# One projection issued ahead of the scores in a windowed-attention loop

## The chip, the cores and the metric

The kernel runs on one core of a Trainium2 chip. The core has five engines that run side by side and meet at semaphores: TensorE for matrix products (its weight loads are listed apart), VectorE, ScalarE, GpSimd, and SyncE, which only issues transfers. The metric is device time in microseconds (us) of one execution, as the median of several.

## The reference

The reference is a decoder of four blocks, each made of a self-attention, a cross-attention and a feed-forward layer, on x of shape 8 x 128 x 128. The change lies in one layer alone, `l1_ffn`, which is itself a small transformer of depth 2 with local attention. Cut to what matters here, each depth computes:

```
h = shift_token(x)                      # second half of the features comes from the token before
q, k, v = split(h @ wqkv)               # 8 heads of 64
q, k = l2norm(q) * qs, l2norm(k) * ksc  # per head
q, k = rotary_xpos(q, k)
o = local_attention(q, k, v)            # windows of 64, each sees itself and the one before
x = x + o @ wo
x = x + gated_ffn(shift_token(x))       # layernorm, w1 (2 x 341), gelu gate, w2
```

The norm of q and k stands ahead of the rotation, and the scores q @ k stand behind it, so each group of tokens goes through a long chain of small operations: projection, squares, their sum, the inverse root, the product with it, rotation, transposition, scores, softmax, values, output projection.

## The kernel before

All twelve layers run one after the other. In `layer_l1_ffn` (line 2888 on) the tokens are cut into 8 blocks of 128 for each of the 2 depths. A loop over steps s = 0 to 7 treats block s, and at the same time prepares the blocks behind it. There is no scheduler: on each engine the instructions run in the order in which the code issues them, and an instruction whose semaphore has not come up holds all that is behind it on that engine. What one step does, by engine:

- TensorE: `turn_qk` (transposes of the rotated q and k, line 3044), `score` (two products that lay the band mask into the banks, line 3056, then the score products, line 3062), `project` twice (q and k of block s + 2, line 3028), `turn_out` (3070), `turn_shifted` (3078), `project_values` (3035), `project_out` (3087), `hand` (3098, 3101), `value` (3112).
- ScalarE: the copy of the turned q and k to memory (3269), for which the score products wait; the squares of the q and k of block s + 2 (`square`, 3208); the copy of the turned output (3216); the exponentials (3281); copies of values and handed rows.
- VectorE: `unite` (3315), which multiplies q and k of block s + 1 with their inverse norms and by that empties the two projection banks; `divide` (3323, 3327) and `add` (3335) of earlier blocks; the row maxima of the scores (3410) and the subtraction of them (3414); `sum_squares` of block s + 2 (3340, 3345); the sum of the rotated halves (3350); `measure` (3356 to 3364).
- GpSimd: the rotation of block s + 1 (2965, 2967) behind `unite`; then the inverse root of the sums of squares of block s + 2 (2998), for which the next step's `unite` waits.

`project(d, b, n)` writes q (n = 0) or k (n = 1) of a block into one bank each, `QK_BANKS[n]`. There is one such bank for q and one for k. So the product for block s + 2 may not start before `unite` has read the one of block s + 1 out of it: that is the wait in lines 3026 and 3027, and `unite` of block s + 1 stands first in VectorE's step s.

At depth 1, step 0 differs: seven dummy products (`keep_clock_bf`, line 134) stand between `turn_qk` and `score`, and a `turn_x` behind the two projections.

Of the kernel before, what the change touches and what calls it, by code (L numbers as in the profile page):

```python
# [26 lines left out]
B = 8  # L27
# [139 lines left out]
def for_heads(bias, n=4):  # L167

    return bias.unsqueeze(1).broadcast_to([bias.shape[0], n, bias.shape[1]])
# [312 lines left out]
class SmallHeads:  # L482
# [44 lines left out]
    def by_head(self, ap):  # L527
        return ap.rearrange("p (h k) -> p h k", h=4)
# [2359 lines left out]
def layer_l1_ffn(core, tag, w):  # L2888
# [54 lines left out]
    with nc.Block(tag, no_gpsimd_drain=True) as block:  # L2943
# [63 lines left out]
        def _(pe):  # L3007

            def turn_x(d, h):
                bank = X_BANK[d][h]  # L3010
                if d == 0:
                    norm.pe(pe, h, bank)
                    pe.wait_ge(norm.turned.sem, norm.half(norm.turned, h))
                else:
                    pe.wait_ge(joined.sem, joined.at(2 * (d - 1) + h))
                    pe.wait_ge(taken.sem, taken.at(hand_at(d, -1)))
                    for b in range(B // 2 * h, B // 2 * (h + 1)):
                        t = nc.tensor.transpose(ps[bank][:, b % 4 * P:(b % 4 + 1) * P], res[:, b, :], core.ident[:, :])
                    t.then_inc(x_turned.sem, x_turned.up())

            def project(d, b, n):
                g = 8 * d + b
                if b % 4 == 0:
                    pe.wait_ge(x_low.sem, x_low.at(2 * d + b // 4))
                    pe.wait_ge(x_high.sem, x_high.at(2 * d + b // 4))
                if g > 0:
                    pe.wait_ge(united.sem, united.at(2 * (g - 1) + n))
                nc.tensor.matmul(ps[QK_BANKS[n]][:, :], core.xnT[:, b * P:(b + 1) * P], wqkv[d][:, n * BANK:(n + 1) * BANK],  # L3028
                                 start=True, stop=True).then_inc(qk_made.sem, qk_made.up())

            def project_values(d, b):
                g = 8 * d + b
                if b == 1:
                    pe.wait_ge(values_out.sem, values_out.at(g - 1))
                nc.tensor.matmul(ps[A_BANKS[0]][:, :], core.xnT[:, b * P:(b + 1) * P], wqkv[d][:, 2 * BANK:3 * BANK],
                                 start=True, stop=True).then_inc(values_made.sem, values_made.up())

            def turn_qk(g):
                for n in range(2):
                    pe.wait_ge(added_half.sem, added_half.at(2 * g + n))  # L3040
                    if g > 0:
                        pe.wait_ge(exped.sem, exped.at(2 * (g - 1) + n))
                    for i in range(4):
                        t = nc.tensor.transpose(ps[T_BANKS[n]][:, i * P:(i + 1) * P], rotated[:, n, i * P:(i + 1) * P],
                                                core.ident[:, :])
                    t.then_inc(qk_turned.sem, qk_turned.up())

            def score(d, b):
                g = 8 * d + b
                pe.wait_ge(values_out.sem, values_out.at(min(g + 1, 8 * d + 7)))  # L3050
                if b >= 3:
                    pe.wait_ge(taken.sem, taken.at(hand_at(d, b - 3)))
                if d > 0 and b == 0:
                    pe.wait_ge(joined.sem, joined.at(2 * d - 1))
                for n in range(2):
                    nc.tensor.matmul(by_head(ps[A_BANKS[n]][:, :]), core.ident_bf[:, :], for_heads(core.band_bf[:, :]),
                                     start=True, stop=False)
                pe.wait_ge(qk_out.sem, qk_out.at(2 * g + 1))
                for i in range(4):
                    for n in range(2):  # L3060
                        rows = slice(K * n, K * n + K)
                        m = nc.tensor.matmul(ps[A_BANKS[n]][:, i * P:(i + 1) * P], qkT[rows, 0, i, :], qkT[rows, 1, i, :],
                                             start=False, stop=(i == 3))
                        if i == 3:
                            m.then_inc(scores.sem, scores.up())

            def turn_out(g):
                pe.wait_ge(normed.sem, normed.at(2 * g + 1))
                for i in range(4):
                    t = nc.tensor.transpose(ps[O_BANKS[0]][:, i * P:(i + 1) * P],  # L3070
                                            o.rearrange("p h k -> p (h k)")[:, i * P:(i + 1) * P], core.ident[:, :])
                t.then_inc(turned_out.sem, turned_out.up())
# [43 lines left out]
            def up(d, h, i):  # L3116
                n, m = chunk_at(d, h, i), WIDTHS[i]
                if n >= 2:
                    pe.wait_ge(gated.sem, gated.at(n - 2))
                pe.wait_ge(taken.sem, taken.at(hand_at(d, (5, 8)[h])))  # L3120
                for part in range(2):
                    mm = nc.tensor.matmul(ps[GATED_BANKS[h][i][part]][0:m, :],
                                          w1[d][:, part * HID + i * P:part * HID + i * P + m], xn2T[:, half(h)],
                                          start=True, stop=True)
                mm.then_inc(up_made.sem, up_made.up())

            def down(d, h):
                pe.wait_ge(gated.sem, gated.at(chunk_at(d, h, CHUNKS - 1)))
                for t in range(4):
                    for i, m in enumerate(WIDTHS):  # L3130
                        mm = nc.tensor.matmul(ps[DOWN_BANK[h]][:, t * P:(t + 1) * P], hT[h][0:m, i, t * P:(t + 1) * P],
                                              w2[d][0:m, i, :], start=(i == 0), stop=(i == CHUNKS - 1))
                mm.then_inc(down_made.sem, down_made.up())
# [5 lines left out]
            for d in range(DEPTH):  # L3139
                if d == 0:  # L3140
                    for b in range(2):
                        for n in range(2):
                            project(d, b, n)
                        project_values(d, b)
                else:
                    turn_x(d, 0)
                    up(d - 1, 1, 0)
                    project(d, 0, 0)
                    project(d, 0, 1)
                    up(d - 1, 1, 1)  # L3150
                    project_values(d, 0)
                    up(d - 1, 1, 2)
                    down(d - 1, 1)
                    project(d, 1, 0)
                    project(d, 1, 1)
                    project_values(d, 1)
                for s in range(B):
                    g = 8 * d + s
                    turn_qk(g)
                    if s == 0 and d > 0:  # L3160
                        core.keep_clock_bf(O_BANKS[1], 7)
                    score(d, s)
                    if s + 2 < B:
                        project(d, s + 2, 0)
                        project(d, s + 2, 1)
                    if s == 0 and d > 0:
                        turn_x(d, 1)
                    if s >= 1:
                        turn_out(g - 1)
                    turn_shifted(g)  # L3170
                    if s + 2 < B:
                        project_values(d, s + 2)
                    if s >= 1:
                        project_out(d, g - 1)
                    if s >= 2:
                        hand(d, s - 2, NEXT_BANK)
                    value(g)
                last = 8 * d + 7
                up(d, 0, 0)
                turn_out(last)  # L3180
                hand(d, 6, LAST_BANK)
                up(d, 0, 1)
                project_out(d, last)
                up(d, 0, 2)
                hand(d, 7, LAST_BANK)
                core.keep_clock_bf(O_BANKS[0], 6)
                down(d, 0)
                hand(d, 8, LAST_BANK)
# [1138 lines left out]
```

## Time and profile before

| | |
|---|---|
| time, median of 3 runs | 1264.51 us (1263.1 to 1265.53) |
| the profiled execution's own time | 1265.53 us |
| its span | 1263.6 us |
| busy over the span: TensorE products | 1132.3 us (90%) |
| TensorE weight loads | 788.6 us (62%) |
| VectorE | 687.9 us (54%) |
| ScalarE | 533.4 us (42%) |
| GpSimd | 472.0 us (37%) |
| mean granted TensorE clock | 0.954 of full |

The span is from the first to the last instruction of the profiled execution; its own time has some 2 us around that. The busy shares are means over twelve layers with different limits, so they say little about one loop. The loop that is changed runs from 519 us (depth 0) and from 627 us (depth 1) after the start of the span. Transfers are few there: the layer's weights were loaded before.

### The profile page before, as it was taken

Reading aid. Unit: us, or ns where it says so; the run is one execution under the profiler, and the core shown is the slowest. Engines: PE = TensorE matmul, PEld = TensorE weight load, DVE = VectorE, ACT = ScalarE, POOL = GpSimd, SP = SyncE. Lnnn points to the kernel's source line nnn. Section 1 sums busy time; section 2 is a strip of 40 time slices with the busy share of each in tenths; the row PEclk is TensorE's granted clock in tenths of the full one; section 3 lists DMA queues with packets and bytes.
Section 4 is the critical chain, followed back from the end, with each engine's and each line's share of the span. In section 5 each row is a group of like instructions: output and inputs, shape, how many; then the busy total and the mean of one; then the engine's idle time right before and its main releaser. Section 6 shows DMA issues by size and latency. Waiting matters only on the chain. (4 is left out here: it accounts for less than half of the span.)

```text
span 1263.6 us, 22906 instructions
## 1 busy us (share of the span) xinstructions
PE 1132.3 (90%) x8793; PEld 788.6 (62%) x8793; DVE 687.9 (54%) x2110; ACT 533.4 (42%) x1374; POOL 472.0 (37%) x547
## 2 busy tenths in 40 slices
PE   5999989999867886798899899989999999988987
PEld 5877867577642254477467666745567775556765
DVE  5555552354449945586478467638722146846402
ACT  5434332366546642355445453304443323443332
POOL 7959730122345622785478250012000012031404
PEclk9999999899996788899999999999999998999989
DMA  5000050532029001000000000000011100010312
GB/s 178 1 5 2 1 217 1 167 85 68 2 104 267 20 2 43 1 1 1 1 1 1 1 10 2 2 11 25 22 55 34 50 16 1 2 38 21 113 37 56
DMA packets 51628, 52.54 MB, mean 42 GB/s; under 512 B 19552, under 2 KB 42336, under 8 KB 50496
## 3 DMA queue, kind: packets, MB, share of 16 engines
q1 hardware_dynamic: 50496, 48.97, 12.4%
q0 software_dynamic: 1024, 2.10, 0.8%
q8 instruction: 71, 1.16, 0.4%
q14 instruction: 37, 0.30, 0.1%
HBM read 43.85 MB, written 7.21 MB: 40 GB/s over the span
## 5 line engine op out<-in xcount | busy, mean ns | idle before, releaser
L471 POOL TENSOR_TENSOR ln_rstd<-ln_ve,ln_half 128x4 f32<-128x4 f32 x28 | 28.5, 1019 | 286.6 <-DVE ln_ve L446 286.4
L664 ACT ACTIVATE scratch<-bank 128x512 f32<-128x512 f32 x96 | 52.3, 595 | 77.1 <-PE bank L555 77.1
L619 DVE TENSOR_REDUCE scratch<-bank 128x4 f32<-128x512 f32 x96 | 61.5, 682 | 16.6 <-PE bank L539 8.8
L1252 ACT ACTIVATE scratch<-bank 128x512 f32<-128x512 f32 x64 | 38.2, 596 | 66.5 <-PE bank L1208 66.4
L2065 POOL TENSOR_TENSOR scratch<-scratch 128x512 f32<-128x512 f32 x32 | 33.2, 1039 | 86.4 <-DVE scratch L2247 86.4
L1218 PEld LDWEIGHTS bank<-weights,scratch 128*128 128x128 f32 x512 | 59.5, 192 | 7.2 <-issue 7.2
L2998 POOL TENSOR_TENSOR scratch<-scratch 128x16 f32<-128x16 f32 x16 | 51.7, 3231 | 32.0 <-DVE scratch L3345 31.9
L1271 DVE SCALAR_TENSOR_TENSOR x_res<-bank,scratch,x_res 128x128 f32<-128x128 f32 x64 | 18.0, 344 | 82.3 <-PE bank L1218 82.3
L625 DVE TENSOR_TENSOR scratch<-bank,scratch 128x512 f32<-128x512 f32 x96 | 61.3, 679 | 0.0
L1208 PE MATMUL bank<-xnT,weights 128*128 128x512 f32 x128 | 59.5, 608 | 0.7 <-ACT xnT L1241 0.7
L1218 PE MATMUL bank<-weights,scratch 128*128 128x128 f32 x512 | 59.6, 275 | 0.0
L539 PE MATMUL bank<-scratch 32*128 32x512 f32 x192 | 52.3, 632 | 1.5 <-DVE scratch L625 1.4
L555 PEld LDWEIGHTS bank<-ident,scratch 128*128 128x128 f32 x384 | 42.0, 141 | 17.6 <-DVE scratch L625 10.6
L555 PE MATMUL bank<-ident,scratch 128*128 128x128 f32 x384 | 51.8, 278 | 0.6 <-DVE scratch L625 0.6
L2200 ACT ACTIVATE scratch<-bank,scratch 128x128 f32<-128x128 f32 x128 | 45.0, 387 | 3.4 <-DVE scratch L2271 3.4
L3551 POOL TENSOR_TENSOR scratch<-scratch 128x1024 f32<-128x1024 f32 (+5 forms) x48 | 42.9, 894 | 3.8
L3546 POOL TENSOR_TENSOR scratch<-scratch 128x2048 f32<-128x2048 f32 x8 | 36.2, 4523 | 16.6 <-DVE weights L1759 16.1
L1505 ACT ACTIVATE scratch<-bank 128x512 f32<-128x512 f32 (+1 forms) x48 | 25.7, 543 | 38.6 <-PE bank L1425 37.5
L1208 PEld LDWEIGHTS bank<-xnT,weights 128*128 128x128 f32 x128 | 23.7, 195 | 25.0 <-issue 23.6
L2271 DVE TENSOR_REDUCE scratch<-bank 128x4 f32<-128x512 f32 x32 | 20.6, 686 | 34.2 <-PE bank L2144 34.2
L3208 ACT ACTIVATE scratch<-bank 128x512 f32<-128x512 f32 x32 | 19.1, 598 | 46.5 <-PE bank L3028 46.5
L3028 PE MATMUL bank<-weights,xnT 128*128 128x512 f32 x64 | 33.4, 646 | 5.8 <-DVE scratch L3315 5.7
(591 smaller groups left out, 2942.1 us busy)
## 6 DMA issues: line engine op xcount, KB each, us to landing
scratch<-conv_kernels SPq DMA_DIRECT2D x8, 1024.0 KB, 11.0
weights<-e_l_ffn_w SPq DMA_DIRECT2D x20, 256.0 KB, 3.0
scratch<-e_l_ffn_w SPq DMA_DIRECT2D x4, 1024.0 KB, 15.3
values<-scratch SPq DMA_DIRECT2D x8, 512.0 KB, 2.7
scratch<-values SPq DMA_DIRECT2D x8, 512.0 KB, 4.4
weights<-w_l_ffn SPq DMA_DIRECT2D x1, 3698.0 KB, 12.4
scratch<-e_l_ffn_w SPq DMA_DIRECT2D x4, 768.0 KB, 6.9
weights<-w_l_attn SPq DMA_DIRECT2D x1, 2560.5 KB, 9.3
```

Of the source, the lines that this page charges most:

```text
L539: s = self.nc.tensor.matmul(self.by_head(self.core.ps[n % 4][:, :]), self.qT[rows, b * P:(b + 1) * P], self.km[rows, :, b * P:(b + 1) * P] ...
L555: t = self.nc.tensor.transpose(self.core.ps[4 + n % 2][:, i * P:(i + 1) * P], self.shift[:, n % 4, i * P:(i + 1) * P], self.core.ident[:, :])
L619: self.nc.vector.tensor_reduce(self.top[:, n % 4, :], self.by_head(self.core.ps[n % 4][:, :]), AX_X, ALU.max, negate=True).then_inc(self.t ...
L625: self.nc.vector.tensor_tensor(self.by_head(self.shift[:, n % 4, :]), self.by_head(self.core.ps[n % 4][:, :]), self.top[:, n % 4, :].unsqu ...
L664: self.nc.scalar.activation(self.prob_of(n), self.by_head(self.core.ps[4 + n % 2][:, :]), ACT.Exp, scale=scale) \
L1208: nc.tensor.matmul(ps[UP_BANKS[i]][:, :], wa[e % 2][:, i * P:(i + 1) * P], core.xnT[:, half(h)], start=True, stop=True).then_inc(up_made.s ...
L1218: mm = nc.tensor.matmul(ps[Y_BANKS[u % 3]][:, t * P:(t + 1) * P], hT[h][:, i, t * P:(t + 1) * P], wb[e % 2][:, i, :], start=(i == 0), stop ...
L1252: nc.scalar.activation(hT[u % 2][:, i, :], ps[UP_BANKS[i]][:, :], act_func) \
L2200: a = nc.scalar.activation(prob[:, r, 4 * i + j, :], ps[S_BANKS[i]][:, j * P:(j + 1) * P], ACT.Exp, bias=top[:, i, j:j + 1], accum_out=tot ...
L2998: nc.gpsimd.tensor_tensor(rn, ss, power, ALU.pow).then_inc(rooted.sem, rooted.up())
L3546: link(tt(prod, z, wa[:, a].unsqueeze(1).broadcast_to([P, R, 2 * N]), ALU.mult))
L3551: link(tt(out, prod[:, :, 0:h], prod[:, :, h:2 * h], ALU.add))
```

## The change

One of the two projections of block s + 2, that of q, is issued ahead of `score` instead of behind it. The one of k stays where it was. Nothing is added or taken away; in step 6 and 7 there is no projection and nothing changes. It holds for steps 0 to 5 of both depths, 12 places.

```diff
                     turn_qk(g)
                     if s == 0 and d > 0:
                         core.keep_clock_bf(O_BANKS[1], 7)
+                    if s + 2 < B:
+                        project(d, s + 2, 0)
                     score(d, s)
                     if s + 2 < B:
-                        project(d, s + 2, 0)
                         project(d, s + 2, 1)
                     if s == 0 and d > 0:
                         turn_x(d, 1)
```

TensorE's order at depth 0, step 0, before. `bank` is a PSUM bank, `scratch` the layer's working memory, `xnT` the turned tokens, `weights` the layer's weights; one row of a projection or a 128x128 product is one call of the code.

```order
L3044 MATMUL bank<-ident,scratch 128x128 x8
L3056 MATMUL bank<-band_bf,ident_bf 128x512 x2
L3062 MATMUL bank<-scratch 128x128 x8
L3028 MATMUL bank<-weights,xnT 128x512 x2
L3078 MATMUL bank<-ident,scratch 128x128 x8
L3035 MATMUL bank<-weights,xnT 128x512
L3112 MATMUL bank<-scratch 128x65 x8
```

And now, the same engine and step:

```order
L3044 MATMUL bank<-ident,scratch 128x128 x8
L3028 MATMUL bank<-weights,xnT 128x512
L3056 MATMUL bank<-band_bf,ident_bf 128x512 x2
L3062 MATMUL bank<-scratch 128x128 x8
L3028 MATMUL bank<-weights,xnT 128x512
L3078 MATMUL bank<-ident,scratch 128x128 x8
L3035 MATMUL bank<-weights,xnT 128x512
L3112 MATMUL bank<-scratch 128x65 x8
```

The product of line 3028 for q went ahead of the mask products and the scores; the one for k is behind them. Steps 1 to 5 of depth 0 and of depth 1 move in the same way.

TensorE's order at depth 1, step 0, where the dummy products of line 134 stand, before:

```order
L3044 MATMUL bank<-ident,scratch 128x128 x8
L134 MATMUL bank<-key_bias,ident_bf 128x512 x7
L3056 MATMUL bank<-band_bf,ident_bf 128x512 x2
L3062 MATMUL bank<-scratch 128x128 x8
L3028 MATMUL bank<-weights,xnT 128x512 x2
L3018 MATMUL bank<-ident,scratch 128x128 x4
```

And now:

```order
L3044 MATMUL bank<-ident,scratch 128x128 x8
L134 MATMUL bank<-key_bias,ident_bf 128x512 x7
L3028 MATMUL bank<-weights,xnT 128x512
L3056 MATMUL bank<-band_bf,ident_bf 128x512 x2
L3062 MATMUL bank<-scratch 128x128 x8
L3028 MATMUL bank<-weights,xnT 128x512
L3018 MATMUL bank<-ident,scratch 128x128 x4
```

The projection for q went behind the dummies and ahead of the mask products and scores. On the other engines no instruction moved.

## Rows read from the trace of the kernel before

**Rows 1.** Busy time by engine, us and (instructions): depth 0, steps 0 to 7.
```profile
core 0: us, PE busy (x) PEld busy (x) DVE busy (x) ACT busy (x) POOL busy (x), PEclk, DMA share, GB/s
519.00:595.00 76.00, 69.07 (x524) 53.07 (x524) 57.98 (x134) 37.40 (x78) 56.21 (x45) 1.00 0.00 1
```

**Rows 2.** Timeline (start, us busy, engine, line, tiles), depth 0, step 5: VectorE, GpSimd.
```profile
569.33 1.29 DVE L3315 TENSOR_TENSOR scratch<-bank,scratch 128x512 f32<-128x512 f32 x2 [0.51 <-POOL scratch L2998]
...
571.42 0.28 DVE L3335 TENSOR_TENSOR scratch<-scratch,bank 128x128 f32<-128x128 f32 x1
...
571.77 1.29 DVE L3410 TENSOR_REDUCE scratch<-bank 128x4 f32<-128x512 f32 x2
...
574.33 1.22 DVE L3340 TENSOR_REDUCE scratch<-scratch 128x16 f32<-128x1024 f32 x1
...
575.84 3.28 POOL L2998 TENSOR_TENSOR scratch<-scratch 128x16 f32<-128x16 f32 x1 [1.49 <-DVE scratch L3345]
...
579.15 1.29 DVE L3315 TENSOR_TENSOR scratch<-bank,scratch 128x512 f32<-128x512 f32 x2 [0.68 <-POOL scratch L2998]
```

**Rows 3.** Timeline, depth 0, step 5: TensorE and ScalarE.
```profile
568.80 1.05 PE L3044 MATMUL bank<-ident,scratch 128*128 128x128 f32 x8
...
569.45 1.07 ACT L3269 COPY scratch<-bank 128x512 f32<-128x512 f32 x2 [1.67 <-PE bank L3044]
...
570.58 1.16 PE L3062 MATMUL bank<-scratch 64*128 64x128 f32 x16 [0.29 <-ACT scratch L3269]
...
571.67 1.98 PE L3028 MATMUL bank<-weights,xnT 128*128 128x512 f32 x4
...
573.49 0.60 PE L3070 MATMUL bank<-ident,scratch 128*128 128x128 f32 x4
573.69 0.60 ACT L3208 ACTIVATE scratch<-bank 128x512 f32<-128x512 f32 x1 [0.26 <-PE bank L3028]
...
578.62 1.04 PE L3044 MATMUL bank<-ident,scratch 128*128 128x128 f32 x8
```

**Rows 4.** Timeline, depth 0, step 0 and the start of step 1.
```profile
519.73 1.28 PE L3044 MATMUL bank<-ident,scratch 128*128 128x128 f32 x8 [1.04 <-DVE scratch L3350]
...
522.46 1.29 DVE L3315 TENSOR_TENSOR scratch<-bank,scratch 128x512 f32<-128x512 f32 x2 [2.17 <-POOL scratch L2998]
...
523.21 1.98 PE L3028 MATMUL bank<-weights,xnT 128*128 128x512 f32 x4 [0.36 <-DVE scratch L3315]
...
523.67 1.28 DVE L3410 TENSOR_REDUCE scratch<-bank 128x4 f32<-128x512 f32 x2
...
530.89 1.29 DVE L3315 TENSOR_TENSOR scratch<-bank,scratch 128x512 f32<-128x512 f32 x2 [2.17 <-POOL scratch L2998]
```

**Rows 5.** Timeline, depth 1: step 0, start of step 1, step 5's reduction.
```profile
630.30 1.29 DVE L3315 TENSOR_TENSOR scratch<-bank,scratch 128x512 f32<-128x512 f32 x2 [2.17 <-POOL scratch L2998]
...
631.87 0.59 PE L3056 MATMUL bank<-band_bf,ident_bf 128*128 128x512 bf16 x2
...
632.39 1.16 PE L3062 MATMUL bank<-scratch 64*128 64x128 f32 x16
...
633.58 1.29 DVE L3410 TENSOR_REDUCE scratch<-bank 128x4 f32<-128x512 f32 x2 [1.99 <-PE bank L3062]
...
641.63 1.29 DVE L3315 TENSOR_TENSOR scratch<-bank,scratch 128x512 f32<-128x512 f32 x2 [2.17 <-POOL scratch L2998]
...
682.52 1.29 DVE L3410 TENSOR_REDUCE scratch<-bank 128x4 f32<-128x512 f32 x2
```

**Rows 6.** Busy time by engine in two stretches around a fall of the clock.
```profile
624.90:628.30 3.40, 1.51 (x7) 0.54 (x6) 2.61 (x4) 1.18 (x3) 1.42 (x2) 0.99 0.00 0
628.30:631.70 3.40, 3.40 (x11) 1.69 (x12) 1.29 (x2) 1.13 (x2) 2.60 (x2) 0.51 0.02 5
```
**Rows 7.** Timeline, depth 0 before step 0: a projection at the low clock.
```profile
513.20 3.78 PE L3028 MATMUL bank<-weights,xnT 128*128 128x512 f32 x4 [5.09 <-DVE scratch L3315]
```

**Rows 8.** Line L3062's own view: idle before it by releaser, us and times.
```profile
  ACT scratch L3269: 16.2, 30
```

## The prediction

> **What bounds the loop now.** I read the busy times first, then the timeline of one step, engine by engine, then the two odd steps at the heads of the depths. Through depth 0's steps TensorE is busy for 69.07 of 76 us, or 91%, at a granted clock of 1.00; VectorE has 76%, GpSimd 74%, the weight loads 70% [rows 1]. By the first figure TensorE is the engine to relieve, and the edit would do that: it puts a product where TensorE stands before the scores.
>
> The timeline says otherwise. Call T the start of a step's `unite` (L3315). In depth 0's step 5 T is 569.33, and the next is 579.15. Between them stands one chain: `unite` to 570.62, `divide`, `add` to 571.70, the row maxima from 571.77, the subtraction, the sum of squares at 574.33, then GpSimd's power from 575.84 to 579.12, which is what the next `unite` waited for [rows 2]. The step is 9.82 us long, and VectorE and GpSimd account for all of it by turns. The row maxima start 0.07 after `add` ends and 1.19 after the first score product (570.58) [rows 2, 3]. So in this step scores and `add` come almost together: the scores have no slack towards VectorE. TensorE is nearly a ring of its own: from row maxima to the next transposes (578.62) 6.85 us, from transposes to row maxima 2.97 (568.80 to 571.77) [rows 2, 3]. Both rings need 9.8 us.
>
> **What the projection waits for.** The bank of q is emptied by the first half of `unite`, the first thing of VectorE's step. In step 0 `unite` starts at 522.46 and the waiting product at 523.21: T + 0.75 [rows 4]. The copies of the turned q and k, which the scores wait for now, are ready at 570.52, T + 1.19 (569.45 + 1.07), and the scores start at T + 1.25 [rows 3]. The projection can't run in the hole for nothing: the hole is from about T + 0.8 to T + 1.25, and the product needs more. Two projections and the passage to `turn_out` take 573.49 - 571.67 = 1.82, so one takes 0.91 [rows 3].
>
> **The new step.** TensorE does matmuls in the order of the code, so what is queued behind the waiting projection is the mask pair, the scores, and behind these VectorE's row maxima. From T: 0.75 for the wait, 0.91 for q's projection, 0.43 for the mask pair, 1.19 from the first score product to the row maxima. Sum: row maxima at T + 3.28. The 0.43 is the pair's 0.59 less the tail of the last; the other bound is 0.52, from the start of the pair to the scores [rows 5]. With it the sum is 3.37. A projection may be 0.86, if 0.1 of the 1.82 is the passage from the scores' weights to the first product's, an estimate; then the sum is 3.23. I take 3.28.
>
> From row maxima to the next T: 579.15 - 571.77 = 7.38 in step 5, and 530.89 - 523.67 = 7.22 in step 0 [rows 2, 4]. The difference is that in step 5 the sum of squares waits for ScalarE's second square (573.69 + 0.60 = 574.29, sum at 574.33) [rows 2, 3]. With the row maxima late this wait goes: k's projection is then done before the subtraction. So 7.22 holds, and a full step is 3.28 + 7.22 = 10.50 us instead of 9.82.
>
> Does TensorE permit 10.50? Its own ring would be: row maxima + 6.85 gives the next transposes at T + 10.13, done by 11.17 (1.04), against q's projection at T + 11.25. It comes first by a little. The ring's old hole, where it stood for the copies, is filled, but it isn't the longer ring any more.
>
> Early steps lose more, because there row maxima came soon after T: in step 0 at T + 1.21 (no `divide` or `add` before them) [rows 4].
>
> **The sum, depth 0.** Before, from step 0's T to step 5's row maxima: 571.77 - 522.46 = 49.31. After: 5 x 10.50 + 3.28 = 55.78. Loss 6.47; bounds 6.1 and 7.0 with 3.23 and 3.37. Steps 6 and 7 have no projection, and TensorE leads them: row maxima + 6.85 + 2.97, as before. Nothing is given back there.
>
> **The sum, depth 1.** In step 0 the dummy products hold the mask pair until 631.87, T + 1.57, so the bank has long been free when the projection's turn comes, and the row maxima are late by the projection alone: 633.58 + 0.91 = 634.49. Before, 641.63 - 633.58 = 8.05 followed; that stays, because `turn_x` behind both projections is where it was. The next T is 642.54. Then 4 x 10.50 + 3.28 to step 5's row maxima: 687.82 against 682.52 [rows 5]. Loss 5.30; bounds 5.0 and 5.8.
>
> Together 11.8 us. No transfer is issued by the moved step, and what follows the layer starts when its last product is joined, so it moves along whole.
>
> **The clock.** In depth 0's step 0 TensorE has the transposes from 519.73 to 521.01 and stood until 519.73; now it would stand again from 521.0 to 523.21 [rows 4]. In 624.90 to 628.30 it was busy 1.51 of 3.40 us, and then the granted clock went from 0.99 to 0.51 for the next 3.4 us, its lower level of 1.2 GHz [rows 6]. The new stretch from 519.7 to 523.2 has 1.3 busy in 3.5, less than that, so a fall is likelier than not. At the low clock two projections took 3.78 against 1.98 us [rows 7, 3]: half the speed. If it caught the projection and the mask pair (0.91 + 0.43 at full speed) it would cost 1.3; with the scores' 1.19 too, 2.5; if it doesn't fall, 0. I take 1.3. In the other steps TensorE stands for about 1 us in 10.5, in two pieces, and the clock should stay. The Trainium skill (TensorE: Matmul & The Clock Gate, HAM oscillation) ties the fall to gaps in which TensorE is idle throughout, longer than the one here. By that rule this term is 0 and the sum 11.8. The trace speaks against it: the fall at 628.3 followed a stretch with 1.51 us of work in it.
>
> **Forecast.** 11.8 + 1.3 = 13.1 us. Against the profiled execution's own 1265.53 us (2 us around its span of 1263.6) that is 1278.6; against the median of 1264.51, 1277.6. The execution read was the slowest of three by 1 us, inside the spread.
>
> **Rivals.**
>
> A. As forecast but with no fall of the clock: 1264.5 + 11.8 = 1276.3; with the low bounds (11.1) 1275.6. For it: I have one fall to go by, and where the stretches of idleness fall may differ by execution. 30%, against 48% for the forecast itself.
>
> B. The clock falls in more steps, since TensorE's share drops from 91% to about 85% and its pauses are longer. Each fall costs 1.3 to 2.5; with three more it is about 1283. Against it: depth 0's step 0 of before, with 0.36 us of pause and a longer one behind it, kept 1.00 [rows 1, 4]. 8%.
>
> C. Faster. TensorE is the bound, and its wait before the scores is filled with useful work. That wait is 16.2 us in 30 cases, weight loads and products counted apart [rows 8]; of the product's own hole about 0.44 us can be saved in a step (0.29 at least, by what stood before the scores) [rows 3]. In 12 steps that is 5.3 us at the most: 1259.2. It decides if q's projection has its bank free when the transposes end, that is if `unite` ended its first half before; in step 5 the transposes end at 569.85 and that half at about 570.0, and the ring of VectorE and GpSimd would have to have slack, which rows 2 deny. The Trainium skill (Perfetto Trace Analysis, Identifying the Most-Contended Engine) says to work on the engine with the highest occupancy, but to judge TensorE by its weight loads and not by its products' busy time. By the products' 91% rival C would hold; by the loads' 70%, below VectorE's 76%, it falls, and the trace agrees with the second half of the rule. 5%.
>
> D. No change: the lateness of the scores is absorbed, since the sum of squares, and with it GpSimd's power, could be limited by the squares and not by the row maxima, and q's square comes earlier now. Then 1264.5, within 2.5. Against it: the sum of squares is behind the row maxima in VectorE's order, and the maxima can't precede the scores. 9%.
>
> **The numbers.** Faster by over 0.2% is C: 0.05. Within 0.2%, some 2.5 us, which is about what these runs can tell from no change, is D: 0.09. Slower is the forecast, A and B: 0.86. The range: from below A, with a few steps costing less than 0.68 (TensorE or VectorE making up half of it in six steps, 2 us; with A's low bound that gives 1273.5, and I allow 2 more), to the forecast with the high bounds of 12.8 and 2.5, 1279.8, and one more fall of the clock: 1271.5 to 1282.
>
> **What would show it.** In the changed profile: row maxima (L3410) waiting for the scores (L3062) in all of steps 0 to 5, at T + 3.2 to 3.4; T to T 10.5 us; a product of L3028 waiting for `unite` in 11 steps; no wait of the scores for the copies (L3269) in those steps; the mask pair right behind a projection. Depth 0's stretch from 522.46 to step 5's row maxima should be 55.8 us or some 57, and depth 1's 57.5. The prediction is wrong if T to T stays at 9.8, if the product starts before T + 0.75, or if the lateness of step 5 is gone by step 7.

## The result

| | before | changed |
|---|---|---|
| median | 1263.19 us (1262.57 to 1265.53, 5 runs) | 1275.11 us (1272.66 to 1277.42, 5 runs) |
| profiled execution's own time | 1265.53 us | 1275.4 us |
| its span | 1263.6 us | 1273.6 us |
| mean granted clock | 0.954 | 0.955 |

The changed kernel takes 1.0095 times as long, with an interval of 1.0078 to 1.0112: 11.9 us slower. The forecast was 13.1 us slower and 1277.6 us.

The page's busy times hardly moved. Products, weight loads, VectorE, ScalarE and GpSimd of the changed kernel:

```profile
PE 1133.1 (89%) x8779; PEld 785.4 (62%) x8793; DVE 688.0 (54%) x2110; ACT 534.7 (42%) x1374; POOL 471.8 (37%) x547
```

The time went into standing, so it has to be looked for in a step. In the changed kernel lines behind 3162 have a number one higher: `unite` is 3316, the row maxima are 3411, the copy of the turned q and k is 3270; in the variants further down they move by a few more. This is the timeline of depth 0, step 5 (start, us busy, engine, line, tiles, idle before), the answer to [rows 2, 3], up to the next `unite`:

```profile
577.14 1.04 PE L3044 MATMUL bank<-ident,scratch 128*128 128x128 f32 x8
...
577.50 1.29 DVE L3316 TENSOR_TENSOR scratch<-bank,scratch 128x512 f32<-128x512 f32 x2 [0.34 <-POOL scratch L2998]
...
578.24 0.30 PEld L3028 LDWEIGHTS bank<-weights,xnT 128*128 128x128 f32 x2 [0.29 <-DVE scratch L3316]
578.24 1.12 PE L3028 MATMUL bank<-weights,xnT 128*128 128x512 f32 x2
...
579.20 0.59 PE L3056 MATMUL bank<-band_bf,ident_bf 128*128 128x512 bf16 x2
...
579.73 1.16 PE L3062 MATMUL bank<-scratch 64*128 64x128 f32 x16
...
580.92 1.29 DVE L3411 TENSOR_REDUCE scratch<-bank 128x4 f32<-128x512 f32 x2 [1.06 <-PE bank L3062]
...
582.87 1.25 PE L3078 MATMUL bank<-ident,scratch 128*128 128x128 f32 x8 [0.48 <-DVE scratch L3415]
...
587.77 1.04 PE L3044 MATMUL bank<-ident,scratch 128*128 128x128 f32 x8
...
588.13 1.29 DVE L3316 TENSOR_TENSOR scratch<-bank,scratch 128x512 f32<-128x512 f32 x2 [0.51 <-POOL scratch L2998]
```

A passage, below, is the time from the start of one operation to the start of the next. With T = 577.50: the projection starts at T + 0.74, the mask pair 0.96 later, the scores another 0.53 later, the row maxima 1.19 behind those. They are at T + 3.42 and now stand 1.06 us for the scores. The next T comes 7.21 later. From T to T it is 10.63 us, where it was 9.82.

Step 0 of depth 0 and the start of step 1, the answer to [rows 4]:

```profile
521.97 1.29 DVE L3316 TENSOR_TENSOR scratch<-bank,scratch 128x512 f32<-128x512 f32 x2 [2.17 <-POOL scratch L2998]
522.71 2.08 PE L3028 MATMUL bank<-weights,xnT 128*128 128x512 f32 x2 [2.20 <-DVE scratch L3316]
524.58 1.06 PE L3056 MATMUL bank<-band_bf,ident_bf 128*128 128x512 bf16 x2
525.57 2.08 PE L3062 MATMUL bank<-scratch 64*128 64x128 f32 x16
...
527.68 1.29 DVE L3411 TENSOR_REDUCE scratch<-bank 128x4 f32<-128x512 f32 x2 [4.43 <-PE bank L3062]
...
534.89 1.29 DVE L3316 TENSOR_TENSOR scratch<-bank,scratch 128x512 f32<-128x512 f32 x2 [2.17 <-POOL scratch L2998]
```

TensorE stood 2.20 us and then did projection, mask pair and scores in 1.87 + 0.99 + 2.11 us, where the full step has 0.96 + 0.53 + 1.19: 2.29 us more. The busy times by engine say why; the figure behind POOL's is the granted clock:

```profile
519.00:522.50 3.50, 1.28 (x8) 0.84 (x8) 1.33 (x3) 1.17 (x2) 2.94 (x1) 0.92 0.00 0
522.50:526.00 3.50, 3.29 (x8) 1.23 (x10) 0.76 (x2) 0.60 (x1) 3.26 (x4) 0.50 0.00 0
```

The clock went from 0.92 to 0.50 of full, the level of 1.2 GHz, behind 3.5 us with 1.28 us of products.

Such a stretch is not always followed by a fall. In depth 1's step 1 of the same execution TensorE stood 2.13 us, with 1.48 us of products in 3.5 us, and the granted clock stayed at 1.00:

```profile
652.41 1.13 PE L3028 MATMUL bank<-weights,xnT 128*128 128x512 f32 x2 [2.13 <-DVE scratch L3316]
```

```profile
648.80:652.30 3.50, 1.48 (x14) 1.24 (x13) 1.33 (x4) 1.07 (x2) 2.83 (x1) 1.00 0.00 0
652.30:655.80 3.50, 3.39 (x22) 1.90 (x23) 2.24 (x8) 0.60 (x1) 3.37 (x4) 1.00 0.00 0
```

Depth 1, the answer to [rows 5]: step 0 and the start of step 1.

```profile
639.46 1.29 DVE L3316 TENSOR_TENSOR scratch<-bank,scratch 128x512 f32<-128x512 f32 x2 [2.17 <-POOL scratch L2998]
...
640.65 1.41 PE L3028 MATMUL bank<-weights,xnT 128*128 128x512 f32 x2
...
643.61 1.29 DVE L3411 TENSOR_REDUCE scratch<-bank 128x4 f32<-128x512 f32 x2 [2.86 <-PE bank L3062]
...
651.66 1.29 DVE L3316 TENSOR_TENSOR scratch<-bank,scratch 128x512 f32<-128x512 f32 x2 [2.17 <-POOL scratch L2998]
```

The row maxima are at T + 4.15, where they were at T + 3.28, and the 8.05 us behind them stayed to the hundredth.

| from step 0's T to step 5's row maxima | before | changed | more | forecast |
|---|---|---|---|---|
| depth 0 | 49.31 | 58.95 | 9.64 | 6.47 + 1.3 |
| depth 1 | 52.22 | 58.24 | 6.02 | 5.30 |

The loop lies between two issues of weight transfers on SP. Before and after, that stretch ("the layer" below) reads:

```profile
499.34 0.35 SPq L4210 DMA_DIRECT2D weights<-w_l_attn  x1
732.14 0.34 SPq L4210 DMA_DIRECT2D weights<-w_l_xattn  x1
```

```profile
498.82 0.35 SPq L4211 DMA_DIRECT2D weights<-w_l_attn  x1
...
747.22 0.35 SPq L4211 DMA_DIRECT2D weights<-w_l_xattn  x1
```

232.8 and 248.4 us: 15.6 more, which is the 9.64 + 6.02 of the table. The span grew by 10.0 only. The difference lies in other layers, whose code is the same. The largest piece, between two other issues of weights, before and then changed (busy times by engine, granted clock behind them):

```profile
1033.26:1113.36 80.10, 77.76 (x631) 46.19 (x631) 58.15 (x128) 29.47 (x59) 15.64 (x16) 0.96 0.02 7
```

```profile
1046.68:1123.67 76.99, 74.59 (x630) 44.29 (x631) 58.18 (x128) 29.48 (x59) 15.64 (x16) 1.00 0.02 7
```

The same instructions, 3.1 us shorter, at a granted clock of 1.00 instead of 0.96. Two more layers took 79.3 instead of 80.6 and 118.6 instead of 120.3 us. Over all profiles of this study these three stayed between 77.0 and 80.2, 79.2 and 80.7, 118.6 and 120.3, with and without the change. So the effect is read from the layer, and the ratio stands beside it. What the layer shows is one execution of each kernel; what the timed runs show is 9.9 to 14.2 us, less than the layer's 15.6.

### The profile page after: what moved, and what is told of

Read it like the earlier page. It is cut to its first block and busy times, and to the rows that moved or that the text cites. A ratio compares the mean times of both kernels' runs of the same rounds, so it can differ in the third digit from the quotient of the medians.

```text
span 1273.6 us, 22892 instructions
## 1 busy us (share of the span) xinstructions
PE 1133.1 (89%) x8779; PEld 785.4 (62%) x8793; DVE 688.0 (54%) x2110; ACT 534.7 (42%) x1374; POOL 471.8 (37%) x547
## 3 DMA queue, kind: packets, MB, share of 16 engines
HBM read 43.85 MB, written 7.21 MB: 40 GB/s over the span
## 5 line engine op out<-in xcount | busy, mean ns | idle before, releaser
L1271 DVE SCALAR_TENSOR_TENSOR x_res<-bank,scratch,x_res 128x128 f32<-128x128 f32 x64 | 18.0, 344 | 80.6 <-PE bank L1218 80.6
L3028 PE MATMUL bank<-weights,xnT 128*128 128x512 f32 x64 | 38.4, 695 | 12.3 <-DVE scratch L3316 12.0
```

## The experiments

Each kernel is compared with runs of the kernel before on the same chip; the ratios below are to those. All layers are from one profiled execution of each.

| kernel | layer us | T0 to row maxima 5: depth 0, depth 1 | ratio to before |
|---|---|---|---|
| before | 232.8 | 49.31, 52.22 | |
| changed | 248.4 | 58.95, 58.24 | 1.0095 (1.0078 to 1.0112) |
| e1 depth 0 only | 242.4 | 58.95, 52.24 | 1.0070 (1.0043 to 1.0097) |
| e2 depth 1 only | 238.7 | 49.31, 58.22 | 1.0031 (1.0015 to 1.0048) |
| e3 not in step 0 | 242.7 | 54.45, 57.07 | 1.0062 (1.0032 to 1.0091) |
| e4 dummies in step 0 | 245.2 | 56.67, 57.51 | 1.0103 (1.0031 to 1.0176) |
| e5 mask pair first | 241.2 | 54.26, 55.83 | 1.0054 (1.0037 to 1.0070) |
| e6 both ahead | 260.4 | 64.84, 64.38 | 1.0230 (1.0190 to 1.0270) |
| e9 wait only | 243.6 | 56.12, 56.22 | 1.0078 (1.0044 to 1.0112) |
| e10 changed again | 248.5 | 58.94, 58.22 | 1.0091 (1.0063 to 1.0120) |
| e11 wait and dummies | 236.0 | 51.81, 53.22 | 1.0003 (0.9982 to 1.0023) |
| e12 four dummies | 232.1 | 49.31, 51.58 | 0.9992 (0.9973 to 1.0010) |
| e7 product for power | 226.0 | | 0.9919 (0.9900 to 0.9938) |
| e8 the same, changed | 232.0 | | 0.9971 (0.9945 to 0.9997) |

**e1 and e2: one depth each.** The edit behind `turn_qk`, with `d == 0` in e1 and `d == 1` in e2:

```diff
+                    if s + 2 < B and d == 0:
+                        project(d, s + 2, 0)
                     score(d, s)
-                    if s + 2 < B:
+                    if s + 2 < B and not (d == 0):
                         project(d, s + 2, 0)
+                    if s + 2 < B:
                         project(d, s + 2, 1)
```

Expected of e1: 

> q's projection goes ahead of the scores in depth 0 only. In the two profiles the layer lasted 232.8 us before and 248.4 after; of the 15.6, depth 0 has 9.6 up to step 5's row maxima, 2.4 of it at a fall of the clock in step 0. Theory (the scores are held by the projection's wait and by the product itself, step by step): the layer lasts 242.4, or 240.0 if the clock doesn't fall there, and depth 1 is as before. Rival (something of the layer as a whole, or of other layers, pays): the layer is not between 239.5 and 243.

Expected of e2: 

> q's projection goes ahead in depth 1 only. Theory: the layer lasts 232.8 + 6.0 = 238.8 us, with depth 0 as before, and the two parts add up to the whole 15.6. Rival: the parts don't add up.

Measured: layer + 9.6 and + 5.9, together 15.5, against 15.6 with both. The depth that wasn't changed kept its 52.2 and 49.3. The loss is local and adds up.

**e3: no move in step 0.** As above, with `s > 0` in place of `d == 0`.

Expected: 

> As the changed kernel, but step 0 of both depths is as before. Theory (early steps lose most, since there the row maxima came soon after unite; and the fall of the clock belongs to step 0's long stand): depth 0 loses 5.1 us instead of 9.6, depth 1 5.1 instead of 6.0, the layer lasts 243.0, the clock stays up in depth 0. Rival (each of 12 steps costs the same): 232.8 + 15.6 x 10/12 = 245.8.

Depth 0 lost 5.14 us without a fall of the clock, the five steps' share. Depth 1 lost 4.85 in an unexpected way. In step 0 the clock now stayed up through mask pair and scores, and the row maxima came at T + 1.61 instead of 3.28; in step 1 it fell:

```profile
640.50:644.00 3.50, 2.19 (x20) 1.95 (x19) 1.39 (x3) 1.27 (x3) 3.24 (x1) 1.00 0.00 0
644.00:647.50 3.50, 2.69 (x4) 0.80 (x4) 2.17 (x6) 0.58 (x1) 2.70 (x4) 0.54 0.00 0
```

There T to row maxima was 4.80 us (644.07 to 648.87), 1.38 more than 3.42. With the five steps' share and the 1.67 by which step 0 was shorter (3.28 - 1.61), that is 5.14 - 1.67 + 1.38 = 4.85. So both the pause in step 0 and the first pause of a moved projection are places where the clock may fall. It need not take either: the changed kernel kept 1.00 behind the same pause of 2.13 us in step 1. What decides is not shown.

**e4: the changed kernel with the clock kept up.** Eight dummies between step 0's transposes and the projection:

```diff
+                    if s == 0 and d == 0:
+                        core.keep_clock_bf(O_BANKS[0], 8)
                     if s + 2 < B:
                         project(d, s + 2, 0)
```

Expected: 

> The changed kernel with eight dummy products of 0.21 us into a free bank in depth 0, step 0, between the transposes and the waiting projection. Theory (TensorE's stand of 2.2 us there lets the granted clock fall, which costs 2.4 us): the clock stays at 1.00, step 0's row maxima come at T + 3.4 instead of T + 5.7, the layer lasts 246.1. Rival (the lateness of step 0 is the order alone): 248.4 stays, or more by the dummies.

Busy times around step 0, and its row maxima:

```profile
517.90:521.40 3.50, 2.63 (x15) 1.59 (x16) 1.39 (x3) 1.44 (x3) 3.25 (x1) 1.00 0.00 0
521.40:524.90 3.50, 3.02 (x23) 1.59 (x22) 1.31 (x3) 0.60 (x1) 2.70 (x4) 1.00 0.00 0
```

```profile
521.45 1.29 DVE L3318 TENSOR_TENSOR scratch<-bank,scratch 128x512 f32<-128x512 f32 x2 [2.17 <-POOL scratch L2998]
...
524.88 1.29 DVE L3413 TENSOR_REDUCE scratch<-bank 128x4 f32<-128x512 f32 x2 [2.14 <-PE bank L3062]
```

The granted clock is 1.00 in both, and the row maxima come at T + 3.43, as in a full step, instead of T + 5.71: the fall had cost 2.28. Depth 1, where nothing was edited, had T + 3.43 too instead of 4.15 (its clock stayed up this time), so the layer is 3.2 shorter and not 2.3. The ratio's interval is too wide to show the gain.

**e5: the mask pair ahead of the projection.** `score` is cut in two; `mask` is its waits for the banks and the mask pair:

```diff
                     turn_qk(g)
+                    mask(d, s)
                     if s + 2 < B:
                         project(d, s + 2, 0)
                     score(d, s)
```

Expected: 

> The changed kernel with the mask pair ahead of q's projection, so that it runs while the projection waits. Theory: T to row maxima falls by 0.5 us, but TensorE's own ring (row maxima + 6.85 to the next transposes, then 0.9 + 0.53 + 0.96 + 1.19 to row maxima) is 10.43 us, so a full step goes from 10.63 to 10.43 only and early steps gain 0.5: the layer lasts 245 us. Rival (only the ring of VectorE and GpSimd binds): 11 x 0.5 less, 242.9.

Shorter than theory and rival had it. Depth 0, step 4 and the start of step 5:

```profile
560.61 1.04 PE L3044 MATMUL bank<-ident,scratch 128*128 128x128 f32 x8
560.98 1.29 DVE L3320 TENSOR_TENSOR scratch<-bank,scratch 128x512 f32<-128x512 f32 x2 [0.51 <-POOL scratch L2998]
561.49 0.59 PE L3056 MATMUL bank<-band_bf,ident_bf 128*128 128x512 bf16 x2
561.92 1.02 PE L3028 MATMUL bank<-weights,xnT 128*128 128x512 f32 x2
562.87 1.16 PE L3065 MATMUL bank<-scratch 64*128 64x128 f32 x16
...
564.06 1.29 DVE L3415 TENSOR_REDUCE scratch<-bank 128x4 f32<-128x512 f32 x2 [0.73 <-PE bank L3065]
...
570.91 1.04 PE L3044 MATMUL bank<-ident,scratch 128*128 128x128 f32 x8
```

The mask pair fills the time until `unite` has freed the bank, and the projection starts at T + 0.94 without a wait. Row maxima at T + 3.08; the step is 10.3 us. Here it is TensorE's own ring that sets it: 3.45 from transposes to row maxima and 6.85 back to the transposes. The pause ahead of step 0's projection was shorter by the mask pair (1.77 us), and the clock didn't fall there. In depth 1's step 1 it did, behind a pause of 1.70 us: to 0.83 and then 0.68 in the next two stretches of 3.5 us, and the step took 10.91 where depth 0's took 10.19. The layer is 7.2 us shorter than the changed kernel's. Some 4.8 of it is the order of the work, 0.3 to 0.4 in each of the 12 steps (T to T 10.20 in depth 0's step 0 and 10.29 in its step 4, against 10.64 in both steps of e4); the rest, some 2.4, is clock: 2.3 and 0.7 that the changed kernel lost in the two steps 0, less the 0.7 lost here.

**e6: both projections ahead of `score`.**

```diff
                     if s + 2 < B:
                         project(d, s + 2, 0)
-                    score(d, s)
-                    if s + 2 < B:
                         project(d, s + 2, 1)
+                    score(d, s)
```

Expected: 

> Both projections go ahead of the scores. Theory (the product's own time is paid once more): T to row maxima 4.4 us, a full step 11.6 instead of 10.63, the layer lasts about 259 us. Rival (the wait for unite is what costs, and it is waited for once only; the squares come earlier): 250 or less.

Depth 0, `unite` of one step, its row maxima, and the next `unite`:

```profile
570.91 1.29 DVE L3315 TENSOR_TENSOR scratch<-bank,scratch 128x512 f32<-128x512 f32 x2 [0.51 <-POOL scratch L2998]
...
575.19 1.29 DVE L3410 TENSOR_REDUCE scratch<-bank 128x4 f32<-128x512 f32 x2 [1.92 <-PE bank L3062]
...
582.40 1.29 DVE L3315 TENSOR_TENSOR scratch<-bank,scratch 128x512 f32<-128x512 f32 x2 [0.34 <-POOL scratch L2998]
```

Row maxima at T + 4.28, next T 7.21 later: 11.49. The second product added its passage of 0.86 to every step and took nothing off elsewhere. The dose doubled and the loss went from 15.6 to 27.6. Falls of the clock are in both. Here the row maxima came at T + 7.21 in depth 0's step 0 and T + 5.97 in depth 1's step 1, 2.9 and 1.7 more than 4.28; in the changed kernel 2.3 and 0.7 (T + 4.15 in depth 1's step 0 against 3.43 in e4) are falls. Without them it is 12.6 and 23.0, and the difference is twelve times 0.87. That confirms the term "one projection, once a step, on the chain".

**e7 and e8: GpSimd's power made short.** In line 2998 `pow` becomes `mult` in the kernel before (e7) and in the changed one (e8), so q and k of both are not normed.

```diff
-                        nc.gpsimd.tensor_tensor(rn, ss, power, ALU.pow).then_inc(rooted.sem, rooted.up())
+                        nc.gpsimd.tensor_tensor(rn, ss, power, ALU.mult).then_inc(rooted.sem, rooted.up())
```

Expected of e7: 

> The kernel before with GpSimd's power (3.27 us for 128 x 16) replaced by a product of the same operands in line 2998, so that q and k are not normed. The bank of q is then free long before TensorE's transposes end. Theory: TensorE's ring of 9.82 us stays the step from step 1 on, and only the heads of the depths get shorter, by two powers in depth 0 and one in depth 1 and some 0.7: the layer lasts about 223 us. Rival (the power is on the only binding ring): a step falls to about 8.7 and the layer to 210.

Expected of e8: 

> The changed kernel with the same replacement of the power, against the kernel before with it. The moved projection has its bank free when the transposes end, which is the condition under which my rival C promised a gain. Theory (the product's time is paid ahead of the scores whatever it waits for, and the hole only moves behind them, where TensorE stands for VectorE's subtraction): TensorE's ring is 10.43 us a step against 9.82, and the layer is about 7 us longer than the one of the kernel before with the product. Rival C: the hole before the scores is filled, 0.3 to 0.44 less a step, the layer 4 to 5 us shorter than it.

The operation took 0.59 us instead of 3.27. The full step of e7 stayed at 9.82 us, as the theory has it and the rival (8.7) has not; its layer took 226.0, 3 us more than expected, and these 3 us were not traced. In the later steps `unite` was no longer late: the bank of q is free when the transposes end. Depth 0 of e8, from step 5's transposes to step 6's:

```profile
565.75 1.04 PE L3044 MATMUL bank<-ident,scratch 128*128 128x128 f32 x8
566.63 1.02 PE L3028 MATMUL bank<-weights,xnT 128*128 128x512 f32 x2
567.49 0.59 PE L3056 MATMUL bank<-band_bf,ident_bf 128*128 128x512 bf16 x2
568.02 1.16 PE L3062 MATMUL bank<-scratch 64*128 64x128 f32 x16
...
569.21 1.29 DVE L3411 TENSOR_REDUCE scratch<-bank 128x4 f32<-128x512 f32 x2 [1.17 <-PE bank L3062]
...
571.15 1.25 PE L3078 MATMUL bank<-ident,scratch 128*128 128x128 f32 x8 [0.48 <-DVE scratch L3415]
...
576.06 1.04 PE L3044 MATMUL bank<-ident,scratch 128*128 128x128 f32 x8
```

The condition of rival C is met: the product stands right behind the transposes, the hole before the scores is gone. Yet the step is 10.31 us, against 9.82 in e7, and e8's layer is 6.0 us longer. The reason is in two differences. From transposes to row maxima it is 3.46 us (2.97 before [rows 2, 3]): the product's 0.86 less 0.36 by which the scores had waited for the copies (0.89 from mask pair to scores in e7, 0.53 in e8). And behind the scores one product less brings nothing, since `turn_shifted` (3078) now stands 0.48 us for the subtraction. In the kernel before it had come last behind two projections without a wait, in step 5 with row maxima at 571.77:

```profile
573.93 1.04 PE L3078 MATMUL bank<-ident,scratch 128*128 128x128 f32 x8
574.80 1.02 PE L3035 MATMUL bank<-weights,xnT 128*128 128x512 f32 x2
```

`project_values` (3035) starts 3.03 us behind the row maxima there, and 3.03 in e8. The hole had been moved from ahead of the scores to behind them.

**e9: the wait without the product.** The kernel before, with TensorE waiting for `unite` ahead of `score`, and both projections behind it:

```diff
+                    if s + 2 < B:
+                        pe.wait_ge(united.sem, united.at(2 * (g + 1)))
                     score(d, s)
```

Expected: 

> The kernel before, but TensorE waits ahead of the scores for the first half of unite, as the moved projection does, while the projection itself stays behind the scores. Theory (of a full step's loss nearly all is the product's time, since the wait ends 0.75 us after T and the scores could start at T + 1.25 anyway): row maxima at T + 2.5, a loss of 1.8 in depth 0 and 0.7 in depth 1, the layer lasts 235.3 us, or 237.6 if the clock falls in depth 0's step 0. Rival (it is the wait that costs): 245 or more.

This expectation failed: the layer took 243.6, and that would have spoken for the rival. The stretches say something else. In steps without a fall the row maxima come at T + 2.48 and the step takes 9.85 us, 0.03 more than before. But steps 0 and 1 of depth 0 and step 1 of depth 1 took 12.7, 11.4 and 12.8. Around depth 0's step 1:

```profile
532.50:536.00 3.50, 1.61 (x13) 1.09 (x12) 1.33 (x3) 1.07 (x2) 2.69 (x2) 0.97 0.02 5
536.00:539.50 3.50, 3.50 (x20) 2.46 (x19) 1.97 (x7) 0.00 (x0) 3.50 (x4) 0.55 0.00 0
```

A wait of 1.9 to 2.2 us of TensorE, and the clock at half behind it. Whether that is all of it was asked of e11.

**e11: e9 with the clock kept up.**

```diff
+                    if s == 0 and d == 0:
+                        core.keep_clock_bf(O_BANKS[0], 8)
+                    if s == 1:
+                        core.keep_clock_bf(A_BANKS[1], 8)
                     if s + 2 < B:
                         pe.wait_ge(united.sem, united.at(2 * (g + 1)))
```

Expected: 

> The wait alone ahead of the scores made the layer 243.6 us long, not the 235.3 that I expected. Its trace shows the clock at its lower level in step 0 of depth 0 and in step 1 of both depths, after stands of 2 us. Here eight dummy products into a free bank stand behind the transposes in depth 0's step 0 and in step 1 of both depths, with the same wait. Theory (the wait costs 2.5 us in itself and the rest of its 10.8 is the clock): T to row maxima 2.5 us in these steps, the layer lasts 235.5. Rival (the wait itself costs that much): 242 or more.

In depth 0 the row maxima come at T + 2.48 in step 0 too (524.65 to 527.13) and at T + 2.59 in step 1, and the layer is 236.0. So the wait alone is worth 3.2 us in the layer; the other 7.6 of e9 were the clock. In the changed kernel with the clock kept up (e4) the same layer is 245.2: the product ahead of the scores is worth 9.2. That is rather too little, since e11 has the low clock of the kernel before in depth 1's step 0 (T + 3.29) and e4 has not.

**e10: the changed kernel once more.**

Expected: 

> The changed kernel once more. In the two profiles the layer cost 15.6 us more but the whole span 10.0, since other layers were shorter (the first by 1.3, l3_attn by 1.7, l3_xattn by 3.1, each with a higher granted clock). Theory (these are falls of the clock that come or stay away from one execution to the next): the layer lasts 248.4 again, within 1, while the others vary. Rival (the change shifts them for good): the same layers are shorter again by the same amounts.

Layer 248.5, and the fall in the same place with the same 2.3 us (row maxima at T + 5.71): the loop's numbers repeat on another chip to 0.1 us. Of the three other layers, two did not repeat: they took 80.6 and 78.7 us, where the changed kernel's first profile had 79.3 and 77.0 and the kernel before 80.6 and 80.1. The third took 118.6 again. So the rival, that the change makes the same layers shorter by the same amounts, does not hold as it stands. The timed loss was again smaller than the layer's, 11.6 us against 15.7.

**e12: a smaller fall in the kernel before.** Four dummies instead of seven in depth 1's step 0:

```diff
-                        core.keep_clock_bf(O_BANKS[1], 7)
+                        core.keep_clock_bf(O_BANKS[1], 4)
```

Expected: 

> The kernel before with four dummy products instead of seven at depth 1, step 0, where the row maxima wait 2 us for the scores held up by the dummies. If the clock behaves as before (low for them, back at the first scores), the row maxima come 1.3 us earlier and the layer lasts 231.5. If the dummies are what brings the clock back, the scores run at the lower level and the layer lasts 232.8 or more. Either way the whole moves by less than 0.2%.

The row maxima came at T + 2.64 (3.28 before), the layer took 232.1 (232.8). That lies between the two values of the expectation and settles neither. The ratio's interval holds 1. No version of this study is measurably faster than the kernel before with the same computation.

## Why the prediction was right, and where its sizes were off

**The bound.** Shown. The step is the ring `unite`, row maxima, power, next `unite`, and with the scores late it lengthens by what they are late: T to row maxima 3.42 and 7.21 behind it, where 3.28 and 7.22 were foretold.

**The wait.** T + 0.75 was right: 0.74 in both steps shown. In step 5 no idle time is recorded ahead of the product, since the end of the transposes, 578.18, is only 0.06 before its start; but its weight load stood 0.29 us for `unite`. From transposes to product it is 1.10 us (577.14 to 578.24), and 0.88 in e8, where the bank is free. So `unite` holds the product by some 0.2 us, and TensorE's ring does come "first by a little".

**The passage.** Mis-sized. One projection took 0.96 to the mask pair instead of 0.91, and the pair 0.53 to the scores instead of 0.43. I had 0.52 as the other bound [rows 5] and took the lower one, an overlap for which there was no row with the scores behind the pair. 0.14 a step in eleven steps (all but depth 1's step 0) is 1.5 us. With it both depths lie above the bounds given for them: 9.64 less the clock's 2.29 is 7.35 against 7.0, and 6.02 against 5.8.

**The clock.** The fall came where it was foretold, and behind less work than [rows 6] shows. The size was 2.29 instead of 1.3: it held through the scores. That is near the upper bound of 2.5. The argument was weaker than it looked, though: depth 1's step 1 also had less work (1.48 of 3.5 us) and kept 1.00. And I had written that in the other steps TensorE stands for about 1 us, where it stood 1.28 us in depth 0's step 1 and 2.13 in depth 1's. Neither was followed by a fall in this execution, for no reason that I had given; e3 shows the price, 1.38. The Trainium skill (TensorE: Matmul & The Clock Gate, HAM oscillation) ties the fall to gaps in which TensorE is idle throughout, longer than the one here. In this trace the gap was 2.20 us, in e9 1.89 to 2.20, and the clock fell. By its rule the layer would have been 2.3 us shorter, as e4's step 0 is. The trace doesn't agree.

**Depth 1.** The 0.91 foretold for step 0 was 0.87, and the 8.05 behind it stayed. But the 0.87 is two errors that cancel, and luck. The projection took 1.24 us to the mask pair (640.65 to 641.89), at a clock still partly low, and it started at T + 1.19, where the pair had started at T + 1.57: the fall came later than in the kernel before, so that the transposes ahead of it took 1.28 us instead of 1.72. The rest, 6.02 - 0.87 = 5.15 against 4.39 foretold, is five times the passage's 0.14.

**The sum.** 9.64 + 6.02 = 15.7 in the loop, 13.1 foretold: some 1.6 of the difference for the passages, 1.0 for the clock. The measured 11.9 came nearer to 13.1 than the loop's 15.7 would have, because the rest of the kernel was shorter by 5.6 us in the execution profiled. That closeness is luck, since nothing of it was foretold. In most experiments, too, the timed effect is smaller than the layer's: 11.6 against 15.7 (e10), 8.9 against 9.6 (e1), 3.9 against 5.9 (e2), 7.9 against 9.9 (e3), 0.4 against 3.2 (e11); in e6 it is larger, 29 against 27.6, and in e4, 13.1 against 12.4. Only in the changed kernel, e10 and e11 among these does the layer's effect lie outside the ratio's interval. Why the rest of the kernel gives time back, and whether by chance or by a rule, stays open.

**The rivals.** A (no fall) is refuted by the two windows of step 0. B (falls in more steps) didn't happen here, but e6 and e9 had two falls and three, so its mechanism is real. D (absorbed) is refuted by 10.63. C is refuted, and my statement of it was wrong: I wrote that it decides if the bank is free when the transposes end. In e8 it is free and the change still costs 6.0 us. What decides is also whether the place that the product is taken from gets shorter by it; there TensorE now waits for the subtraction. I had read TensorE's ring from row maxima to transposes, 6.85, as work; it holds a dependence on VectorE that begins to show once a projection is gone. The Trainium skill (Perfetto Trace Analysis, Identifying the Most-Contended Engine) says that the busy time of the products is no good measure of how near TensorE is to its peak, and that its weight loads are to be looked at. The trace agrees so far: products were busy 91% and weight loads 70% [rows 1], and filling the hole ahead of the scores in e8 made no step shorter.

## What to carry to other kernels

Before a product is moved into a hole of the busiest engine, ask what stands behind it there in order, and which other engine begins its chain with that: here 0.96 us of matmul went ahead of the scores, on which VectorE's and GpSimd's ring depends, and every step paid it, while the place it came from was filled by a wait. If something has to wait at that place, put work ahead of it that is free to run (the mask pair in e5, 7.2 us back in the layer, some 2.4 of them by the clock). And look at every new pause of TensorE at the head of a loop for the clock behind it: one cost 2.3 us, as much as three steps of the edit itself.

## What the runs showed of the hardware

- Pauses of TensorE of 1.89, 2.13 and 2.20 us were followed by a granted clock of 0.50 to 0.55 (the changed kernel, e3, e6, e9), and one of 1.70 us by 0.83 and 0.68 (e5, depth 1). One of 1.77 us (e5, depth 0) was not, and neither was the one of 2.12 or 2.13 us in depth 1's step 1 of the changed kernel, e2, e4 and e10, where the clock stayed at 1.00. So the length of the pause alone doesn't decide; what does is not shown.
- The pause of 2.20 us in depth 0's step 0 was followed by a fall in all five profiles that had it (the changed kernel, e1, e6, e9, e10). Eight bf16 dummies in it, 1.7 to 1.9 us in the trace, kept the clock at 1.00 and the row maxima at T + 3.43 and T + 2.48 (e4, e11).
- A fall can come in one place or in another without an edit there: in e3 depth 1's step 0 is as in the kernel before, yet its clock stayed up, where it had been 0.51 [rows 6], and fell in step 1.
- A wait can cost more than twice as much by the clock as by itself (e9: 7.6 and 3.2 us).
- GpSimd's power on 128x16 took 3.27 us, a product of the same shape 0.59.
- Layers with the same code differ from one profile to the next: the three named above by 1.5 to 3.2 us, and the one just ahead of the changed layer by 5.3 (128.7 us in e5, 134.1 in e7, at granted clocks of 0.78 and 0.76). For effects of a few us the stretch in question is the better measure, and the whole the test of whether it matters.
